# Graph convolution rows and residual loop with features on partitions: weights stationary, scale and bias per partition

## The reference

```
xn = _layernorm(x)
# convolution: dinv = rsqrt(degree), s = x_n times dinv[src], summed over edges (A s)
out = segment_sum(h[src] * dinv[src] * dinv[dst], dst) + conv_bias     # h = xn @ W
mu = out.mean(); xc = out - mu; std = sqrt((xc * xc).mean())           # over all nodes and features
y = xc / (std + EPS) * ln_weight + ln_bias                             # per feature
gnn = where(y >= 0, y, prelu_a * y)
x = x + gnn + mix(xn)                                                  # mix: the attention
xn2 = _layernorm(x) * gamma + beta                                     # statistics per node
logits = xn2 @ Wr + br                                                 # 8 experts, top 2
```

## Time and profile before

| what | us |
| --- | --- |
| median of 3 runs (lowest to highest) | 1373.26 (1373.19 to 1373.59) |
| span of the profiled execution | 1377.2 |
| end of aggregation to first row product | 786.4 to 789.9 |
| rows pass, start of the first product to the last DVE row | 789.9 to 837.1 |
| join, to the first product of the loop | 844.7 |
| residual loop, first to last `finish` | 850.5 to 922.6 |
| busy over the span: PE / DVE / POOL / ACT | 1245.3 / 962.4 / 854.3 / 539.3 |

### The profile page before, as it was taken

One profiled execution on the slowest core, in us unless ns is written; L12 is line 12 of the kernel. 1 busy time (PEld: TensorE's weight loads), 2 busy tenths in 40 slices (PEclk: granted clock), 3 DMA queues, 4 the chain that ended last, 5 costly groups with the idle time before them and its releaser, 6 DMA issues. The chain is left out here.

```text
span 1377.2 us, 30864 instructions
## 1 busy us (share of the span) xinstructions
PE 1245.3 (90%) x8354; PEld 1106.3 (80%) x8355; DVE 962.4 (70%) x2966; ACT 539.3 (39%) x1443; POOL 854.3 (62%) x836
## 2 busy tenths in 40 slices
PE   4997688999899999999898797985799999999998
PEld 4984687887788888887787686873699999999997
DVE  8998787887888777778693288998444444444444
ACT  7707301222333333333311101446455555555553
POOL 1294677777777777777777202431376666666665
PEclk9999899999999999999999898995799999999999
DMA  7005333335666666789898400449244444444443
GB/s 245 0 0 183 111 106 103 107 105 172 194 194 199 198 191 202 207 246 277 260 288 261 144 1 16 138 155 318 64 77 66 68 71 69 72 69 70 71 69 42
DMA packets 138148, 186.89 MB, mean 136 GB/s; under 512 B 21438, under 2 KB 116468, under 8 KB 137916
## 3 DMA queue, kind: packets, MB, share of 16 engines
q0 software_dynamic: 43440, 90.29, 28.7%
q1 hardware_dynamic: 94604, 95.40, 21.8%
HBM read 153.16 MB, written 33.41 MB: 135 GB/s over the span
## 5 line engine op out<-in xcount | busy, mean ns | idle before, releaser
L740 POOL DMA_INDIRECT RG<-table,srci x484 | 477.3, 986 | 153.0 <-issue 149.4
L757 PEld LDWEIGHTS ps<-S_t,RG 128*128 128x128 f32 x1936 | 259.2, 196 | 39.0 <-DMA RG<-table,srci 28.6
L757 PE MATMUL ps<-S_t,RG 128*128 128x96 f32 x1936 | 266.4, 278 | 21.6 <-DMA RG<-table,srci 21.1
L780 PE MATMUL ps<-zrow,R 128*128 128x256 f32 (+1 forms) x784 | 221.1, 389 | 15.2 <-DMA zrow<-table 8.7
L2010 POOL DMA_INDIRECT out<-R,S_t x105 | 166.3, 1584 | 99.5 <-DVE R L1980 55.8
L1893 PE MATMUL ps<-R,RG 128*128 128x128 f32 x1680 | 207.3, 277 | 0.0
L1893 PEld LDWEIGHTS ps<-R,RG 128*128 128x128 f32 x1680 | 198.3, 194 | 0.4 <-issue 0.4
L1903 PE MATMUL ps<-R 128*128 x840 | 198.5, 379 | 0.0
L1014 DVE TENSOR_TENSOR R<-R,ps 128x245 f32 (+4 forms) x300 | 142.1, 474 | 73.7 <-PE ps L768 52.5
L1926 ACT ACTIVATE R<-ps,RG 128x128 f32<-128x128 f32 x420 | 120.0, 368 | 175.8 <-PE ps L1893 175.8
L1976 DVE TENSOR_TENSOR R<-ps,R 128x256 f32<-128x256 f32 x105 | 44.6, 425 | 200.8 <-PE ps L1903 200.8
(11 more groups left out here) (360 smaller groups left out, 1989.9 us busy)
## 6 DMA issues: line engine op xcount, KB each, us to landing
zrow<-table SPq DMA_DIRECT2D x384, 128.0 KB
RG<-table,srci POOLq DMA_INDIRECT x484, 3.3
ntable<-R SPq DMA_DIRECT2D x12, 516.0 KB
table<-RG SPq DMA_DIRECT2D x12, 512.0 KB, 2.9
out<-R SPq DMA_DIRECT2D x12, 512.0 KB, 3.2
R<-in_x SPq DMA_DIRECT2D x6, 896.0 KB, 11.7
R<-in_w SPq DMA_DIRECT2D x8, 514.0 KB, 6.4
slot<-in_x SPq DMA_DIRECT2D x32, 128.0 KB
```

What stands on the lines that cost most here:

```text
L740: nc.gpsimd.indirect_dma_start(out=grows[:, s, :], out_offset=None, in_=table, in_offset=bass.IndirectOffsetOnAxis(ap=srci[:, ND + q, c:c ...
L757: last = nc.tensor.matmul(window(q % 2)[:, h, :], grows[:, s, h * P:(h + 1) * P], S_t[:, q % 2, c, :], start=c == 0, stop=c == GC - 1)
L780: nc.tensor.matmul(psD[:, 0:D], adj[b % 2][0:n, j, :], zrow[0:n, i % ZR, :], start=j == 0, stop=j == T - 1).then_inc(z_used, 1)
```

## The change

**Aggregation stage.** SP stores `dinv` into a DRAM row `degrow` at the stage's start (6,272 elements of 4 bytes), and loads cbias, lnw and lnb as columns (feature on partition) into `cols`. These three loads at the end go away. At the step where `q + 2` is `USED[7] + 3`, among the last dense block, SP loads degrow spread over all 128 partitions into `dinvB` (25,088 bytes each, 3.21 MB), in the half of `R1` that the block before has left; its two waits are on work that earlier loads of the queue have waited for. `dslow` moves to the other half.

**Rows pass.** gw is stationary, acc moves, in spans of 512 nodes: 12 spans and one of 106. DVE multiplies the PSUM by dinvB, in place over acc, and takes bn_stats along the nodes. Weight, scale, bias and statistics are now per partition. The pass leaves acc holding the product.

**Join.** Two `bn_aggr` of 78 values in place of one of 288 and one of 6; `aw` and `bx` are 128x2; no wx. A sign `sgn` and a slope `lower` are computed besides.

**Residual loop.** ACT forms `shifted` per pair of tiles from acc by scale and bias (two Identity of 128x256) and `sloped` (a Relu of 128x512 with scale `lower`); POOL adds both (`prelu`, 128x512); PE transposes each tile back (`turn_back`); DVE adds it from PSUM to the row (`finish`). flip and logits stay, at s-2 and s-3. The PSUM copy `flipped` is ACT's for even tiles and DVE's for odd ones. The join of the row statistics per tile gives way to seven 128x49 operations after the loop.

```diff
-        dslow = R1[:, 0:NC].rearrange("p (g c) -> p g c", c=GC)
+        dslow = R1[:, T * P:T * P + NC].rearrange("p (g c) -> p g c", c=GC)
         gw = RG[:, 4 * D:6 * D].rearrange("p (k n) -> p k n", k=KC)
-        cbias, lnw, lnb = (RG[:, k * D:(k + 1) * D] for k in (6, 7, 8))
+        dinvB = R1[:, 0:NP]
+        cbias, lnw, lnb = (cols[:, k * KC:(k + 1) * KC] for k in range(3))
...
+                sp.dma_start(degrow.rearrange("(t p) -> p t", p=P), dinv[:, :], allow_slow_non_contiguous=True).then_inc(row_out, 16)
+                for d_, s_ in ((cbias, a_cb), (lnw, a_lnw), (lnb, a_lnb)):
+                    sp.dma_start(d_, s_.rearrange("(k p) -> p k", p=P), allow_slow_non_contiguous=True).then_inc(late, 16)
+                sp.wait_ge(row_out, 16)
                 for q in range(-2, GQ - 2):
+                    if q + 2 == USED[NDB - 1] + 3:
+                        sp.wait_ge(z_used, (NDB - 1) * T)
+                        sp.wait_ge(blk_t, NDB - 1)
+                        sp.dma_start(dinvB, degrow.unsqueeze(0).to_broadcast([P, NP])).then_inc(row_in, 16)
                     for b, j in products(q + 2):
                         z_rows(b, j)
                     for t in share(q + 2, D0, D1, T):
...
                 sp.wait_ge(pe_done, GQ - 2)
                 sp.dma_start(gw, a_gw.rearrange("(k p) n -> p k n", p=P)).then_inc(late, 16)
-                sp.dma_start(cbias, a_cb.unsqueeze(0).to_broadcast([P, D])).then_inc(late, 16)
-                sp.dma_start(lnw, a_lnw.unsqueeze(0).to_broadcast([P, D])).then_inc(late, 16)
-                sp.wait_ge(pe_done, GQ - 1)
-                sp.dma_start(lnb, a_lnb.unsqueeze(0).to_broadcast([P, D])).then_inc(late, 16)
                 sp.wait_ge(late, 16 * 4)
+                sp.wait_ge(row_in, 16)
...
+        aw, bx, sgn, lower = small[:, 40 + NX:42 + NX], small[:, 52:54], small[:, 20:21], small[:, 21:22]
+        tot2 = small[:, 24:26]
...
+        vring = slot[:, :, :].rearrange("p (s a) f -> p s (a f)", s=2)
+        aring = zrow[:, 2:6, :].rearrange("p (s a) f -> p s (a f)", s=2)
+        pring = RG[:, 4 * D:8 * D].rearrange("p (s f) -> p s f", s=2)
...
-                    for k in range(KC):
-                        last = nc.tensor.matmul(ps[t % 4][:, 0:D], acc[:, k, t * P:(t + 1) * P], gw[:, k, :],
-                                                start=k == 0, stop=k == KC - 1)
+                def rows(c):
+                    lo, hi = c * SPAN, min((c + 1) * SPAN, N)
+                    if c >= 2:
+                        pe.wait_ge(y_ok, c - 1)
+                    for f in range(KC):
+                        for k in range(KC):
+                            last = nc.tensor.matmul(ps[c % 2 * KC + f][:, 0:hi - lo], gw[:, k, f * P:(f + 1) * P],
+                                                    acc[:, k, lo:hi], start=k == 0, stop=k == KC - 1)
                     last.then_inc(pr_ok, 1)
 
...
-                def scaled(t):
+                def turn_back(t):
+                    pe.wait_ge(p_ok, t // 2 + 1)
                     if t >= 2:
-                        pe.wait_ge(v_ok, t - 1)
+                        pe.wait_ge(x_ok, t - 1)
                     for k in range(KC):
-                        last = nc.tensor.matmul(psW[t % 2][:, 0:D], acc[:, k, t * P:(t + 1) * P], wx[:, k, :],
-                                                start=k == 0, stop=k == KC - 1)
-                    last.then_inc(px_ok, 1)
+                        last = nc.tensor.transpose(psP[t % 2][:, k * P:(k + 1) * P],
+                                                   pair(pring, t // 2)[:, k, t % 2 * P:(t % 2 + 1) * P], ident[:, :])
+                    last.then_inc(p_ps, 1)
 
                 def flip(t):
                     pe.wait_ge(x_ok, t + 1)
                     if t >= 2:
-                        pe.wait_ge(f_ok, t - 1)
...
-                for s in range(T + 5):
+                for s in range(T + 3):
                     if s < T:
-                        scaled(s)
-                    if 0 <= s - 4 < T:
-                        flip(s - 4)
-                    if 0 <= s - 5 < T:
-                        logits(s - 5)
+                        turn_back(s)
+                    if 0 <= s - 2 < T:
...
+                def shifted(i):
+                    if i >= 2:
+                        act.wait_ge(p_ok, i - 1)
+                    here = pair(vring, i)
+                    for k in range(KC):
+                        last = act.activation(here[:, k, :], acc[:, k, i * PAIR:min((i + 1) * PAIR, NP)], ACT.Identity,
+                                              scale=aw[:, k:k + 1], bias=bx[:, k:k + 1])
+                    last.then_inc(v_ok, 1)
+
+                def sloped(i):
+                    act.wait_ge(v_ok, i + 1)
+                    act.activation(pair(aring, i), pair(vring, i), ACT.Relu, scale=lower).then_inc(av_ok, 1)
...
                 def flipped(t):
                     act.wait_ge(f_ps, t + 1)
                     if t >= 2:
                         act.wait_ge(l_ps, t - 1)
-                    act.activation(turned[:, t % 2, :], psF[t % 2][:, 0:D], ACT.Copy).then_inc(f_ok, 1)
-
-                for s in range(T + 4):
-                    if s < T:
-                        negative(s)
-                    if 0 <= s - 4 < T:
-                        flipped(s - 4)
+                    act.activation(turned[:, t % 2, :], psF[t % 2][:, 0:D], ACT.Copy).then_inc(f_ok[t % 2], 1)
+
+                act.wait_ge(bx_ok, 1)
+                for i in range(NPAIR + 3):
+                    if i < NPAIR:
+                        shifted(i)
+                        sloped(i)
+                    if 0 <= i - 3 < NPAIR:
+                        flipped(2 * (i - 3))
 
...
-                def residual(t):
-                    pool.wait_ge(v_ok, t + 1)
-                    nc.gpsimd.tensor_tensor(o_tile(t), o_tile(t), halved(shift[:, t % 4, :]), ALU.add).then_inc(xa_ok, 1)
-
-                for t in range(T):
-                    residual(t)
+                def prelu(i):
+                    pool.wait_ge(av_ok, i + 1)
+                    if i >= 2:
+                        pool.wait_ge(p_ps, 2 * (i - 1))
+                    nc.gpsimd.tensor_tensor(pair(pring, i), pair(aring, i), pair(vring, i), ALU.add).then_inc(p_ok, 1)
+
+                for i in range(NPAIR):
+                    prelu(i)
...
+                def rows(c):
+                    lo, hi = c * SPAN, min((c + 1) * SPAN, N)
+                    v.wait_ge(pr_ok, c + 1)
+                    for f in range(KC):
+                        last = nc.vector.tensor_tensor(acc[:, f, lo:hi], ps[c % 2 * KC + f][:, 0:hi - lo], dinvB[:, lo:hi],
+                                                       ALU.mult)
+                    last.then_inc(y_ok, 1)
+
+                def row_stats(c):
+                    lo, hi = c * SPAN, min((c + 1) * SPAN, N)
+                    v.wait_ge(y_ok, c + 1)
+                    for f in range(KC):
+                        last = nc.vector.bn_stats(ystat[:, f, c, :], acc[:, f, lo:hi])
+                    return last
+
...
-                ch.done(nc.vector.bn_aggr(pm, stats[:, 0:T - 1, :].rearrange("p t s -> p (t s)")))
-                ch.done(nc.vector.bn_aggr(tm, stats[:, T - 1, :]))
-                v.wait_ge(sh_ok, 2)
-                ch.done(nc.vector.tensor_tensor(tot2, means, share_of, ALU.mult))
+                for f in range(KC):
+                    last = nc.vector.bn_aggr(small[:, 32 + 2 * f:34 + 2 * f], ystat[:, f, :, :].rearrange("p c s -> p (c s)"))
+                ch.done(last)
+                ch.done(nc.vector.tensor_tensor(tot2, means, cbias, ALU.add))
...
-                ch.done(nc.vector.tensor_scalar(aw, lnw, d2, None, ALU.mult))
-                ch.done(nc.vector.tensor_tensor(wx, gw, aw.unsqueeze(1).to_broadcast([P, KC, D]), ALU.mult))
-                v.sem_inc(wx_ok, 1)
+                ch.done(nc.vector.tensor_scalar(aw, lnw, d2, sgn, ALU.mult, ALU.mult))
                 ch.done(nc.vector.scalar_tensor_tensor(bx, cbias, mu, aw, ALU.subtract, ALU.mult))
-                ch.done(nc.vector.tensor_tensor(bx, bx, lnb, ALU.add))
...
+                ch.done(nc.vector.scalar_tensor_tensor(bx, lnb, sgn, bx, ALU.mult, ALU.add))
+                v.sem_inc(bx_ok, 1)
 
                 def finish(t):
-                    v.wait_ge(ng_ok, t + 1)
-                    v.wait_ge(xa_ok, t + 1)
-                    nc.vector.scalar_tensor_tensor(halved(o_all[:, t, :]), halved(minus[:, t % 4, :]), a1, o_tile(t),
+                    v.wait_ge(p_ps, t + 1)
+                    nc.vector.scalar_tensor_tensor(halved(o_all[:, t, :]), halved(psP[t % 2][:, 0:D]), sgn, o_tile(t),
                                                    ALU.mult, ALU.add).then_inc(x_ok, 1)
 
                 def x_stats(t):
                     v.wait_ge(x_ok, t + 1)
                     nc.vector.bn_stats(stats[:, t, :], o_all[:, t, :]).then_inc(st_ok, 1)
 
```

(35 more changed lines are left out.)

98 lines of the change are left out of this document (39 added, 59 removed).

## The result

The changed kernel takes 1427.47 us (median of 4 runs, 1425.92 to 1428.82); the kernel before, in the runs beside it, 1373.42. The ratio is 1.0377, 95% interval 1.0357 to 1.0397: 54 us slower. It lies 5.5 us above the top of the forecast range, and 16.5 above the forecast itself. One of the runs of the kernel before beside the last experiments took 3917 us and stands in no comparison here.

The account below looks back on a forecast made before the run. Before: PE bounds the rows pass and experts, PE and DVE the loop; gathers, DMA and PE are close in the aggregation. 6.5 - 2.0 + 31.3 + 1.4 = +37.2 on 1373.3 gives 1411 us, range 1376 to 1422.

Parts of the forecast that it names:

- The early store: Aggregation: storing dinv and loading three columns costs 0, at most +0.5 us, since SP's first rows are needed much later.
- The broadcast load: Aggregation: loading 3.21 MB ahead of seven row loads costs +6.5 us (3.1 to 11.7), lost clock included.
- spare time: Aggregation: idle DMA time to the stage's end, 4.8 us; half of it, 2.4, was taken to hide the load.
- Rows pass, join, first finish: From first row product to first finish: PE still sets the pass's pace; -2.0 us with pass +0.4 and join -0.7 included.
- Loop: Residual loop, first to last finish: 103.4 us in place of 72.1 at half clock, +31.3 us (+23.7 to +36).
- the chain: Residual loop: successive PE and DVE steps for two tiles at half clock, sum 4.47 us, 2.24 a tile.
- rival 1: Residual loop: finish still waits for POOL, at half clock; about +6.6 us, 1417 in all; chance 0.12.
- the third rival: Whole kernel: the clock rises in the loop and DMA hides the load as far as possible; 1369.2 us; chance 0.10.
- The half clock: Residual loop: PE starts at half clock and stays there throughout; PEclk between 0.45 and 0.6.
- 950 to 965: Evidence for half clock, kernel before: PE busy 14.70 of 15 us with small products, clock staying at 0.50.
- The stretch of transposes from 116 to 136 us: Evidence against half clock, kernel before: PE did transposes, busy 17.67 of 20 us, at clock 1.00.
- After the loop: Last finish to the operation on all variances: seven 128x49 operations +1.1 us, last logits +0.3, together +1.4.

Follow-up runs that it names:

- both: Changed kernel with the broadcast load in 13 pieces in the rows pass and dinv transposed by PE, stored in 49 pieces of 512 bytes: 1405.56 us, ratio 1.0226.
- flat_store: Changed kernel with the early dinv store in 128 pieces of 196 bytes, nodes in another order: 1417.89 us.
- in_pass: Changed kernel with the broadcast load moved out of the aggregation, in 13 pieces of 512 columns at the rows pass's start; early store unchanged: 1418.67 us.
- thin: Kernel before with the residual loop's second product cut from 256 to 64 columns per record: 1394.1 us, ratio 1.0127.
- late: Changed kernel with the logits of a tile one step later on PE (s-4 in place of s-3): 1399.5 us, ratio 1.0183.
- fill: Changed kernel with two spare products 128x256 per tile added to the residual loop on PE: 1420.09 us, ratio 1.0328.
- best1: hold with one spare product 128x256 per tile added in the loop: 1367.91 us, ratio 0.9954.
- hold: both with late's logits one step later, and eight spare products 128x384 around the join, none in the loop: 1377.91 us, ratio 1.0030.
- best2: best1 with the seven 128x49 statistics operations put ahead of DVE's last PSUM copy: 1366.79 us, ratio 0.9927.

## Why the prediction was right and wrong

**The time.** Forecast 1411, range to 1422; measured 1427.5. The sum failed in one term, the aggregation, 12 us too low by the table, and 15.8 by what both took away (22.3); the others came within 2.1 us each and partly cancelled.

**The early store: the step that failed.** The prediction put "0, at most +0.5", on the ground that SP's first rows are not needed for tens of microseconds. I looked at who waits for SP's queue and not at what the store does to the DMA engines, which POOL's gathers share. Its 6,272 pieces of 4 bytes held them for 23.7 us (an estimate from this: 23.7 x 16 / 6,272 = 60 ns of one engine's time for each piece, with the gathers' packets counted in), the gathers that POOL issued from 142.8 on came late, PE waited for the first of them until 165.9, and POOL waited 8.7 us for PE. In pieces of 196 bytes the same store landed in 1.5 us (flat_store). The runs give it 10.5 us at the stage's end (flat_store against the changed kernel) to 11.8 (both against in_pass), of 16.6 at its start.

**The broadcast load: right mechanism, size too low.** Forecast 6.5 (3.1 to 11.7); measured 10.5 (in_pass against the changed kernel) to 11.8 (both against flat_store), at the upper bound, and 5.1 to 8.2 for half of the bytes. What failed is the 2.4 us (up to 4.8) of "spare time" that I let the DMA give back. None of it came back: the wait of PE for table rows behind the load in the queue was 11.68 us in one block, and the stage ended later by as much. The landing took 14.2 us where I had 7.9 to 10.3.

**Rows pass, join, first finish.** -2.4 against -2.0. The pass itself ran as argued, PE-bound; DVE's four operations of 512 columns took 2.6 us a span by the profile's timeline (1.29 for two), inside PE's 3.44. The prediction's count of products is off by a factor that cancels: four products of 512 columns (eight records) stand in place of eight of 256 (16 records) for four tiles. From the bias to the first `finish` it was 4.1 us, as forecast.

**Loop.** +29.2 against +31.3, PEclk 0.50 throughout, a steady pair in 4.38 us where the chain gave 4.47. The step in it that was high is the logits: four products were spaced by 0.71 at half clock, not 0.80 (913.92 to 914.63 in the timeline above). These 0.09 a pair, 24 times, make up the 2.1 us. `finish` took 483 to 485 ns, also the 25 that ran while POOL's operation (1.29) did, so rival 1 was rightly set aside. The Trainium skill (SBUF — State Buffer, "SBUF: two separate sides") says that DVE waits for GpSimd only in a two-port mode or with two inputs from SBUF; `finish` now reads one of its inputs from PSUM, and the trace agrees. (Where the prediction says beside this page that the third rival falls away, it is the first that does.)

**The clock.** The half clock was called rightly, on little evidence. Of that, 950 to 965 was the stretch to trust: PE records nearly without gaps, products of 105 columns, half clock. thin and late are the same picture with PE records filling 80.00 of 80.00 and 65.00 of 65.00 us at 0.50; fill and best1 have gaps and run at 1.00. All that thin takes from the loop before, and all that fill adds to the changed kernel's loop and best1 to hold's, are columns of 256-column products. The Trainium skill (TensorE: Matmul & The Clock Gate, "Part 4: PE-mode transpose") says that transposes do not bring the full clock; the loops with transposes and logits alone agree (0.50 in late, and in hold from 845 on). The stretch of transposes from 116 to 136 us, at 1.00 in the earlier trace rows, is no rise either: the clock of the kernel before was already at 1.00 ahead of it, under other products:

```profile
100.00:112.00 12.00, 7.48 (x71) 6.42 (x69) 8.66 (x17) 1.10 (x3) 6.54 (x11) 1.00 0.00 0
112.00:136.00 24.00, 21.67 (x98) 10.41 (x97) 23.31 (x71) 23.35 (x48) 9.54 (x24) 1.00 0.72 242
```

So transposes alone kept the full clock there for 24 us, while hold lost it within some 2.5 us of its first transposes. Why, no run here tells.

**What I took for the cause.** The prediction says "so the question is which clock they get". It was half of it: late has the same clock and is 27 us faster in the loop. The chain was in my working, as a sum, but I did not ask which link was there by the order of the program alone.

**After the loop.** +3.2 against +1.4. The seven operations take 1.26 us from the first to the operation on all variances (970.99 to 972.25). Ahead of them stand DVE's last copies, which wait for PE's transposes: 3.1 us from the last `finish` to the first of the seven. The half clock is the smaller part of this, for in best1, at the full clock, it is still 2.5 (908.51 to 911.01; its logits are one step later). best2 shows that the last copy among them is worth 0.6. The prediction had 0.3 for all that stands there.
